# Layer 0 of a four-layer graph kernel: totals turned in 32x32 blocks, pairwise sums, mixed values copied by ScalarE, three of 32 units a round masked by VectorE

## The reference, cut to what matters

```python
q = x1.reshape(n, 8, -1).transpose(1, 0, 2) * SCALE
k, vv = (a.reshape(n, 8, -1).transpose(1, 0, 2) for a in (x2, v))
scores = jnp.einsum('hnd,hmd->hnm', q, k)
scores = jnp.where(adj > 0, scores, NEG_FILL)
attn = jax.nn.softmax(scores, axis=-1)
out = jnp.einsum('hnm,hmd->hnd', attn, vv)
```

## Time and profile before

| | us |
|---|---|
| median of 3 runs | 873.53 |
| the profiled execution, own time | 873.28 |
| its span | 871.6 |
| TensorE busy in the span | 814.6 (93%) |
| VectorE busy | 688.7 (79%) |
| ScalarE busy | 581.2 (67%) |
| TensorE busy in 200 to 300 us | 98.14, granted clock 1.00 |
| VectorE busy in 200 to 300 us | 93.03 |
| ScalarE busy in 200 to 300 us | 69.94 |

### The profile page before, as it was taken

The page is one execution under the profiler, slowest core; times in us unless marked ns, Lnnn a source line. Parts: engine busy times, 40 slices in busy tenths (PEclk is TensorE's granted clock), DMA queues, the critical chain, the costliest instruction groups (busy, mean ns, idle before and its releaser), DMA issues. The chain is left out here.

```text
span 871.6 us, 18880 instructions
## 1 busy us (share of the span) xinstructions
PE 814.6 (93%) x7820; PEld 510.7 (59%) x7820; DVE 688.7 (79%) x1045; ACT 581.2 (67%) x608; POOL 149.4 (17%) x287
## 2 busy tenths in 40 slices
PE   3999999999999999995869999999988999999997
PEld 1344444344444444442559999999944557777786
DVE  7587979898998989896889999999853595555454
ACT  6798989896777767671479999999959731111000
POOL 3501012653110100000520000000001352111122
PEclk9999999999999999997979999999998999999999
DMA  8965354393211010002121110011000000000011
GB/s 292 263 196 165 110 149 131 109 242 88 84 25 49 13 49 1 13 1 66 42 100 52 52 40 30 34 51 52 3 1 1 1 1 1 1 1 1 2 49 49
DMA packets 28183, 56.85 MB, mean 65 GB/s; under 512 B 5760, under 2 KB 9984, under 8 KB 26560
## 3 DMA queue, kind: packets, MB, share of 16 engines
q1 hardware_dynamic: 23968, 46.19, 17.2%
q0 software_dynamic: 4128, 9.44, 4.1%
HBM read 38.70 MB, written 2.23 MB: 47 GB/s over the span
## 5 line engine op out<-in xcount | busy, mean ns | idle before, releaser
L484 ACT ACTIVATE ex<-scores_ps,shift 128x1024 f32<-128x1024 f32 x256 | 262.5, 1130 | 77.3 <-PE scores_ps L344 69.4
L555 DVE TENSOR_TENSOR esum<-esum,ex 128x1024 f32<-128x1024 f32 x192 | 223.0, 1212 | 6.1 <-ACT ex L484 6.1
L340 PE MATMUL scores_ps<-qst,kst 128*128 128x512 f32 x512 | 201.6, 475 | 2.5 <-ACT ex L484 1.8
L994 PE MATMUL banks<-fx,pos 128*128 128x132 f16 x2048 | 161.7, 223 | 9.4 <-DVE fx L1097 5.4
L1262 ACT ACTIVATE steps<-a_all,big_b_head 128x2048 fp8e5<-128x2048 f32 x87 | 166.2, 1988 | 0.0
L344 PE MATMUL scores_ps<-edge,negI 128*128 128x512 fp8e5 x512 | 155.3, 385 | 0.0
L340 PEld LDWEIGHTS scores_ps<-qst,kst 128*128 128x128 f32 x512 | 90.2, 189 | 69.6 <-ACT ex L484 18.2
L994 PEld LDWEIGHTS banks<-fx,pos 128*128 128x128 fp8e5 x2048 | 122.2, 98 | 11.5 <-issue 8.4
L1001 PE MATMUL banks<-fm,edge 128*128 128x66 f16 x2048 | 104.8, 194 | 0.0
L1001 PEld LDWEIGHTS banks<-fm,edge 128*128 128x128 fp8e5 x2048 | 87.3, 98 | 0.0
L1166 DVE TENSOR_TENSOR pos<-steps,edge 128x1024 int32<-128x1024 int32 (+1 forms) x65 | 76.9, 1203 | 11.1 <-PE banks L994 5.5
(11 more groups left out here) (209 smaller groups left out, 933.4 us busy)
## 6 DMA issues: line engine op xcount, KB each, us to landing
adj_raw<-in_adjT_dram SPq DMA_DIRECT2D x32, 512.0 KB, 5.2
a_all<-score_rows_dram SPq DMA_DIRECT2D x8, 1024.0 KB, 4.6
kst<-high_low SPq DMA_DIRECT2D x56, 64.0 KB, 4.5
kst<-high_low POOLq DMA_DIRECT2D x56, 64.0 KB, 4.9
qst<-high_low POOLq DMA_DIRECT2D x56, 64.0 KB, 2.2
qst<-high_low SPq DMA_DIRECT2D x56, 64.0 KB, 3.6
ex<-in_x2T_dram SPq DMA_DIRECT2D x2, 1024.0 KB, 6.8
ex<-in_xT_dram SPq DMA_DIRECT2D x2, 1024.0 KB, 8.8
```

The costliest lines, as they stand in the source:

```text
L340: nc.tensor.matmul(to, kst[:, h, jt * P:(jt + 1) * P], qst[:, it % 2, h, :], start=True, stop=False)
L484: nc.scalar.activation(ex[:, s % ER, h, :], scores_ps[:, u % SR, :], ACT.Exp, bias=shift[:, it // NC * HG + h:it // NC * HG + h + 1], scal ...
L555: nc.vector.tensor_tensor(esum[:, h, :], other, ex[:, s % ER, h, :], ALU.add).then_inc(summed, 1)
L994: done = nc.tensor.matmul(place(half, i), pos[:, group_of(h, k, half) % GR, jt % GU, i * P:(i + 1) * P], fx[:, e, jt].rearrange("p k r c - ...
```

## The change

Four edits in `attention`, all in layer 0.

1. `keep` becomes `close` with 5 pieces. VectorE turns the totals in 32x32 blocks (`transpose`), so that the 512 totals of a head stand in 16 columns. The limit, the least value and the reciprocal then work on 128x16, and a second block transpose, reading each column 32 times, spreads them again.
2. ScalarE copies the mixed values (`keep_mixed`), behind the last exponential of `jp` 0 and ahead of that step's conversions.
3. `add` takes two heads in one instruction of 128x2048, at h 1 and 3, but in the last step.
4. At `jp` 2, 4 and 6 the unit of head 0 gets no products with `edge` on TensorE. VectorE multiplies its exponentials with (edge == 0) instead (`veil`), just ahead of that step's adds. Mixes, adds and flips wait for it.

```diff
+    VEILED = (2, 4, 6)
@@ TensorE
-                    for t in range(2):
+                    for t in range(0 if bare else 2):
                         last = nc.tensor.matmul(to, negI[:], edge[:, jt, columns(it % NC)], start=False, stop=True)
...
                     pe.wait_ge(exp_ready, HG * (s + 1))
+                    if jp in VEILED:
+                        pe.wait_ge(veiled, veils_to(s))
@@ ScalarE
+                def keep_mixed(it):
+                    act.wait_ge(mixed, (it + 1) * JP)
+                    nc.scalar.copy(yT[:, it // NC, columns(it % NC)], mixed_ps).then_inc(stored, 1)
...
+                        if jp == 0 and it and h == HG - 1:
+                            keep_mixed(it - 1)
                         ...
                         if s and s % 2 == 0 and h == HG - 1 and s + AHEAD < CONVERTED:
                             convert(s + AHEAD)
                             convert(s + AHEAD + 1)
@@ VectorE
+                    nc.vector.tensor_tensor(esum[:, hh, :], other, ex[:, s % ER, hh, :], ALU.add).then_inc(summed, count)
+                def veil(s):
+                    dve.wait_ge(exp_ready, s * HG + 1)
+                    at = ex[:, s % ER, 0, :].rearrange("p (t n) -> p t n", t=2)
+                    nc.vector.scalar_tensor_tensor(out=at, in0=edge[:, 2 * jp:2 * jp + 2, columns(it % NC)], scalar=0.0,
+                                                   in1=at, op0=ALU.is_equal, op1=ALU.mult).then_inc(veiled, 1)
...
+                def close(it, piece):
                     if piece == 0:
-                        dve.wait_ge(mixed, (it + 1) * JP)
-                        nc.vector.tensor_copy(yT[:, g, at], mixed_ps).then_inc(stored, 1)
+                        dve.wait_ge(totals, it + 1)
+                        nc.vector.transpose(turned, total_ps).then_inc(recip_step, 1)
+                    elif piece == 1:
+                        nc.vector.tensor_scalar(compact[:], turned.rearrange("p (b r) -> p b r", r=DH)[:, :, 0], TRUST / 2, None,
+                                                ALU.max).then_inc(recip_step, 1)
+                        nc.vector.tensor_reduce(out=least[:], in_=compact[:], axis=AX.X, op=ALU.min).then_inc(lowest, 1)
                         nc.vector.tensor_tensor(low, least[:], low, ALU.min).then_inc(lowest, 1)
+                        nc.vector.reciprocal(compact[:], compact[:]).then_inc(recip_step, 1)
+                    elif piece == 2:
+                        nc.vector.transpose(recip, compact[:].unsqueeze(2).broadcast_to([P, CW // DH, DH])).then_inc(recip_step, 1)
+                    elif piece == 3:
                         nc.vector.tensor_tensor(yT[:, g, at], yT[:, g, at], recip, ALU.mult).then_inc(closed, 1)
...
+                        if h == 0 and jp in VEILED:
+                            veil(s)
+                        if s == STEPS - 1:
+                            add(s, h, 1)
+                        elif jp and h % 2:
+                            add(s, h - 1, 2)
+                        elif it and not jp:
                             halve(it - 1, h)
```

More of the change, by code:

```diff
@@ L109, in attention @@
     QUADS = {"k": ((0, 2), (1, 3)), "q": ((0, 1), (2, 3))}
-    PIECES = 4
+    CLOSING = 4
+    VEILED = (2, 4, 6)
     ER = 3
@@ L144, in attention @@
         least = S.sb("least_sum", [P, 1], fp32)
+        compact = S.sb("distinct_sums", [P, CW // DH], fp32)
         parts = S.sb("high_low", [P, HL, 2, CW], fp32r)
@@ L199, in adds_before, with veils_to @@
             return it * ADDS + (jp - 1) * HG + h + 1
+        def veils_to(s):
+            it, jp = s // JP, s % JP
+            return it * len(VEILED) + sum(v <= jp for v in VEILED)
         with nc.Block() as block:
@@ L326, in score @@
                     it, jp, u = s // JP, s % JP, s * HG + h
-                    g = it // NC
+                    g, bare = it // NC, h == 0 and jp in VEILED
                     if h == 0:
@@ L339, in score @@
                         to = scores_ps[:, u % SR, t * CW:(t + 1) * CW]
-                        nc.tensor.matmul(to, kst[:, h, jt * P:(jt + 1) * P], qst[:, it % 2, h, :], start=True, stop=False)
-                    for t in range(2):
+                        last = nc.tensor.matmul(to, kst[:, h, jt * P:(jt + 1) * P], qst[:, it % 2, h, :], start=True, stop=bare)
+                    for t in range(0 if bare else 2):
                         jt = 2 * jp + t
@@ L497, in _ @@
                             convert(s + AHEAD + 1)
+                keep_mixed(ROUNDS - 1)
             @block.vector
@@ L562, in halve @@
                                             ).then_inc(halved, 1)
-                def keep(it, piece):
-                    g, at = it // NC, columns(it % NC)
-                    step = Chain(dve, recip_step, it * (PIECES + 1))
+                def close(it, piece):
+                    g, at, done = it // NC, columns(it % NC), it * CLOSING
                     if piece == 0:
-                        dve.wait_ge(mixed, (it + 1) * JP)
-                        nc.vector.tensor_copy(yT[:, g, at], mixed_ps).then_inc(stored, 1)
+                        dve.wait_ge(totals, it + 1)
+                        nc.vector.transpose(turned, total_ps).then_inc(recip_step, 1)
@@ L570, in keep @@
                     elif piece == 1:
[L571 to L575, removed]
+                        dve.wait_ge(recip_step, done + 1)
+                        nc.vector.tensor_scalar(compact[:], turned.rearrange("p (b r) -> p b r", r=DH)[:, :, 0], TRUST / 2, None,
+                                                ALU.max).then_inc(recip_step, 1)
@@ L633, in _ @@
                     for h in range(HG):
-                        if jp:
-                            add(s, h)
-                        elif it:
+                        if h == 0 and jp in VEILED:
[5 more added lines that the diff above has]
+                        elif it and not jp:
                             halve(it - 1, h)
@@ L640, in _ @@
                         piece = (jp - 1) * HG + h
-                        if it and 0 <= piece <= 4 + PIECES:
-                            keep(it - 1, piece)
+                        if it and 0 <= piece <= CLOSING:
+                            close(it - 1, piece)
                         if W_AT + 2 <= s < W_AT + 4:
@@ L652, in _ @@
                             flip(it - NC - 1, (jp - 4) * 2 + h // 2)
-                for piece in range(5 + PIECES):
-                    keep(ROUNDS - 1, piece)
-                    if piece == 2:
+                for piece in range(CLOSING + 1):
+                    close(ROUNDS - 1, piece)
+                    if piece == 1:
+                        dve.wait_ge(lowest, ROUNDS * 2)
                         nc.vector.tensor_scalar(fine[:], low, TRUST, None, ALU.is_ge).then_inc(fine_made, 1)
-                    if piece == 2 + PIECES:
+                    if piece == 3:
                         dve.wait_ge(counted, 1)
```

36 lines of the change are left out of this document (18 added, 18 removed).

## The result

The changed kernel takes 873.07 us (median of 20 runs, 871.55 to 874.21), the kernel before 874.13 in the same comparisons (20 runs). The ratio is 0.9983, 95% interval 0.9975 to 0.9991: 1.5 us faster. The forecast was 2.9 us, so the sign is right and the size is about half. The time lies inside the forecast's range of 867 to 876 us, and the change is smaller than the 0.3% that the forecast had put at the edge of what can be told.

A forecast was written before the change was run, and what follows sets the result against it. Batches were taken as bound by ScalarE's unbroken exponentials with three score slots, round ends by late VectorE. Copy +1.9, VectorE -1.9 and layer 0's end -2.9 gave -2.9 us, from 873.53 to 870.6; range 867 to 876.

The forecast's parts named there:

- Masks on TensorE: Layer 0 batches: dropping two of four products in 24 units gains 0; upper bound 11.0 us.
- Copy on ScalarE: Ends of rounds 0, 1 and 2: conversions queued behind the copy make the next exponential 0.62 late, +1.9 us.
- rival with late tiles: Rounds 1 to 3: late conversions make later tile loads late, one to two us more, 872.5; chance 0.08.
- Closing chain: End of layer 0, last totals to last add's start: 5.85 us becomes 3.3, a gain of 2.5.
- rival of two passes: VectorE's block transpose of 4-byte values costs two passes: +0.7 us, 874.3; chance 0.13.
- VectorE's account: VectorE's work per round changes by -0.6 us, removing lateness in rounds 3, 5, 6 and 0.6 in round 4: -1.9.
- The start: VectorE's first add of a round now needs two exponentials: +1.0 us a round.
- Last adds: End of layer 0: the last add, which releases the totals, comes 0.4 us earlier with 12 pairs.
- The masks free TensorE: Layer 0: if the run of exponentials gave way, 24 x 0.46 = 11 us more gain, 859.6; chance 0.09.
- VectorE becomes the bound through the masks: Layer 0 rounds: a mask at 2.28 us makes each round 2.8 later, +18 on the forecast, 889; chance 0.07.
- margin of 0.1 us a round: VectorE's room before the first loss; beyond it each 0.1 us of a mask costs 1.5 us.

The follow-up runs named there:

- e2: Changed kernel with no masked units, all products with the marks back on TensorE; ratio 0.9922 to the kernel before.
- e3: Changed kernel with head 3, the last unit of its step, masked instead of head 0; ratio 1.0033 to the kernel before.
- e1: Changed kernel with ScalarE's copy of the mixed values moved behind the two conversions; ratio 0.9967 to the kernel before.
- e4: Changed kernel with each mask issued ahead of the second pair of adds of the step before; ratio 0.9979 to the kernel before.
- e8: Changed kernel with one add for each head instead of pairs; ratio 1.0009 to the kernel before.
- e10: Kernel before with only the masks added (head 0 at jp 2, 4 and 6); ratio 1.0411 to the kernel before.
- e7: Kernel before with only the closing over turned totals; single adds, copy on VectorE, no masks; ratio 0.9922 to the kernel before.
- e9: e6 with two masks a round, at jp 2 and 4; ratio 0.9909 to the kernel before.
- e5: Changed kernel without masks and with the copy behind the conversions, e1 and e2 together; ratio 0.9907 to the kernel before.
- e6: e5 with one mask a round, on the last unit of jp 2; ratio 0.9865 to the kernel before.

## Why the forecast was half right

**Masks on TensorE, 0: right.** Plain batches stay at 11.09 (after) and 11.08 (e2). The eighth unit hangs on the fifth exponential, which ScalarE's unbroken run fixes. e3 adds the condition: the gain is hidden only while an exponential stands behind the short unit.

**Copy on ScalarE, +1.9: right**, +1.88, and e1 takes it back. Of the rival with late tiles the changed kernel shows no cost beyond it.

**Closing chain, -2.5: right in mechanism**, -2.81. The block transpose takes 0.72 us out of PSUM and 0.71 in SBUF. The Trainium skill ("VectorE: DVE Perf Modes", "The three transpose paths") carried on to this size gave an estimated 0.7, which the trace now bears out; the rival of two passes is dead. A pair takes 2.20 us in a run, (8.89 - 2.29) / 3, and saves 0.07 against two single adds, as forecast. The 0.16 us that the formula of the Trainium skill (the same page, "The TRN2 errata") would have made of it are not in the trace.

**VectorE's account, -0.6 a round and -1.9 in all: the step that failed.** It gave -0.13 a round (44.50 to 44.37) and -0.57 in all (0.10 in round 3, 0.16 in round 4, 0.15 and 0.16 in rounds 5 and 6). So the waits before the totals of these rounds stayed, where the forecast had none in rounds 3, 5 and 6. The terms that were mis-sized:

- *A mask is not always an add's 1.14 in the queue.* Directly ahead of the add that reads it, it holds 1.42. The waits by releaser show this place 12 times, 2.8 us in all (columns: us in total, times, longest; the longest is the first mask of all):

```profile
DVE esum L572 <- DVE ex L578: 2.8, 12, 0.6
PEld mixed_total_ps L386 <- DVE half_sum L585: 6.4, 7, 2.1
```

  e4 shows it by moving the mask: 1.14 again. In round 6 one of three masks stands so, +0.28; with single adds behind the masks (e8, e10) it would be 0.17 each. The forecast took its duration, which was right, and left out what the dependent instruction behind it adds.
- *The add behind a removed reciprocal was cheap*, 1.08 us (321.80 to 322.88) and not 1.14; so with the four reciprocals 4 x 0.06 = 0.24 less went away than was put down; VectorE's work from first add to last halves fell by 1.20 us (42.14 to 40.94), not by 1.6.
- *The start* moved by 1.07, not 1.0.
- *The minimum behind the least value* was left out of the account, to the good: it held the queue 0.20 us before (317.66 to 317.86) and 0.07 after (317.75 to 317.82), -0.13.

Together 0.46, which is the 0.47 that is missing. None of them is large. What made the sum fragile is that the rounds turned on the small difference of 6.2 us taken away and 5.7 added, and that the masks alone were 3.4 of the latter. e2 and e7 say what that difference hid: without the masks the same edits are worth 6.8 us.

**Last adds, -0.4: wrong**, 0. The last totals start 1.58 us later than before, just what the last batch is late (388.79 to 390.37). It hung on the same account: -0.13, and two pairs fewer, which gives back 2 x 0.07.

**The sum** with the measured terms: +1.88 - 0.57 + 0 - 2.81 = -1.50, with -1.23 - 0.17 = -1.40 read at the next stage's first product, and -1.5 by the ratio of all runs. The next stage's first product was forecast for 405.5 and came at 407.15. That the two spans are equal (871.6 and 871.7) is this one pair of executions: 1.35 us went behind layer 0, in code that is the same in both, as the last section shows.

**The rivals.** "The masks free TensorE" and "two passes for a transpose" are refuted. "VectorE becomes the bound through the masks" was put as a doubled price of 2.28; that didn't happen (1.13 to 1.42 us a mask), but its direction did: the forecast gave a margin of 0.1 us a round before the first loss, and the 0.28 of one mask used up more than that. It didn't become slower because the closing chain alone brings 2.8.

## What to carry to other kernels

Work that leaves an engine off the bound frees time only where its successor waits for nothing else: find the last thing that the batch waits for, and shorten what comes behind that. Before giving new work to an engine that has just been relieved, try the relief alone; here it was worth 6.8 us, and the work put in its place ate 5.3. Price an instruction in a queue by the distance to the next start, with the reader that follows and its size, and put a copy that waits for another engine behind the work that waits for nothing.

## What the runs showed of the hardware

**TensorE's clock fell only behind long waits, but not behind all of them.** In layer 0, ahead of its last products, every fall to half clock in these traces lasted 3.41 us and stands behind a wait of TensorE of 2 us or more. In e3 it fell behind waits of 2.20 us (round 3) and 2.06 us (round 6), in e10 behind or at the end of five waits of 2.85 to 4.17 us, in e1 in the first batch behind one of 3.06 us for an exponential. In e3 the batches behind took 1.23 and 1.59 us more. But waits of 2.14 us (round 5) and 1.97 us (the weights' sum) in e3 and of 3.32 us (the weights' sum) in e10 had no such sequel, nor had those of the changed kernel (up to 1.24 us inside the rounds). So the length of a wait doesn't decide alone, and what else does is not shown here. The last totals can be hit as well: in e3 the clock was at half from 402.99 on, behind a wait of 3.11 us, and these products took 2.97 us instead of 1.92.

**The code behind layer 0 is the same in all runs, and its time isn't.** From the next stage's first product to the last product of the stages that end the kernel, the traces show 455.4 to 458.3 us (before 456.38, after 457.73, e7 455.39, e9 458.34). Two places of low clock go with part of it. First where the next stage begins, windows of before and of after:

```profile
408.00:412.00 4.00, 3.62 (x11) 2.84 (x12) 1.39 (x5) 0.64 (x2) 0.82 (x2) 0.51 0.60 174
```

```profile
407.00:412.00 5.00, 4.84 (x14) 3.73 (x15) 1.39 (x5) 0.73 (x3) 1.61 (x4) 0.50 0.70 213
```

Half clock until 412 in both: the changed kernel starts the stage 1.23 us earlier and spends that time at half clock, and the stage's first 40 us, to its first product with `pos` (L994 in before, L1023 in after), take 40.98 us instead of 40.23. Then from 640 to 700 us, of before (after has the same 0.94) and of e7:

```profile
640.00:700.00 60.00, 52.98 (x225) 26.39 (x224) 27.31 (x83) 47.17 (x83) 14.22 (x30) 0.94 0.01 1
```

```profile
640.00:700.00 60.00, 54.14 (x228) 26.93 (x229) 33.07 (x97) 45.89 (x83) 19.11 (x39) 0.97 0.01 1
```

0.94 is two stretches of 3.41 us at half clock, 0.97 is one. From the first product with `before_in_tile` (L1710 in the kernel before) to the end of the last product, traces with one (e1, e5, e7, e8, e10) take 226.2 to 226.6 us, those with two (before, after, e2, e3, e4, e6, e9) 227.1 to 228.2. What decides between one and two stays open. A forecast from one trace can therefore miss a single execution by a microsecond or more, and a difference of that size between two spans says nothing of a change in layer 0.
